# Experts right behind attention: one routing table of 71 tiles with two lists, the last 28 rows routed ahead of them, row buffers that also hold results

## What is computed (the reference, cut)

```
x = x + L0_conv(_ln_c(x))          # gated attention over image rows, 64 channels, 128 x 128, 4 heads of 32
t = _to_tokens(x)                  # 8192 tokens of 128 numbers
t = t + L0_ffn(_ln_t(t))           # 8 experts, 2 for each token

def _L0_ffn_ref(x, Wg, bg, W1, b1, W2, b2):
    gate_logits = xf @ Wg + bg
    top_w, top_i = jax.lax.top_k(gate_logits, 2)
    top_w = jax.nn.softmax(top_w, axis=-1)
    ...
    for e in range(E):
        h = jax.nn.gelu(xf @ W1[e] + b1[e], approximate=False)      # 128 -> 512
        out = out + w_dense[:, e:e + 1] * (h @ W2[e] + b2[e])       # 512 -> 128
```

## Time and profile before

| | |
|---|---|
| runs | 858.76 us median of 3 (855.01 to 860.4) |
| profiled execution | 861.2 us, span 859.0 us, mean granted clock 0.917 |
| busy | PE 670.5 (78%), DVE 632.3 (74%), ACT 614.8 (72%), POOL 418.4 (49%) |
| the chain that ended last | PE 49%, DVE 19%, issue 8%, POOL 8%, ACT 7%, DMA 6% |

### The profile page before, as it was taken

How to read it: one execution, slowest core, us unless ns; L and a number is a source line. 1 busy time by engine, 2 the same in 40 slices (tenths; PEclk the granted TensorE clock), 3 DMA queues, 4 the chain that set the end, 5 groups by cost and what they waited for, 6 DMA issues and landing times.

```text
span 859.0 us, 23093 instructions
## 1 busy us (share of the span) xinstructions
PE 670.5 (78%) x7161; PEld 551.0 (64%) x7162; DVE 632.3 (74%) x2324; ACT 614.8 (72%) x1550; POOL 418.4 (49%) x516
## 2 busy tenths in 40 slices
PE   0098988888999899789885162799888888999980
PEld 0097777776777677677674152587666667888860
DVE  4973688885778987687985557677667767899974
ACT  2673999997998898688897231587767666888860
POOL 7010122235436465445665630177777777566660
PEclk9999999998999998899997555799999999999995
DMA  9968300000000000000011320223223323543557
GB/s 207 266 173 187 56 2 2 2 2 2 2 1 2 2 27 17 12 17 27 27 33 35 94 75 17 44 82 85 84 80 84 89 84 92 159 133 96 159 157 266
DMA packets 65925, 63.97 MB, mean 74 GB/s; under 512 B 21158, under 2 KB 57064, under 8 KB 64298
## 3 DMA queue, kind: packets, MB, share of 16 engines
q1 hardware_dynamic: 54170, 34.90, 16.6%
q0 software_dynamic: 9152, 18.76, 6.5%
q10 hardware_dynamic: 2512, 9.18, 3.9%
HBM read 35.88 MB, written 26.93 MB: 73 GB/s over the span
## 4 chain that ended last, share of the span: by engine, by line
PE 49%; DVE 19%; issue 8%; POOL 8%; ACT 7%; DMA 6%; SPq 1%; ACTq 0%; POOLq 0%; DVEq 0%
PE PT L1552 9%; PE PT L1390 5%; PE S L1378 4%; PE S L1535 3%; POOL expert_out L774 3%; POOL routed L743 3%; PE B L1335 3%; ACT L L850 3%; PE S L1537 3%; PE S L1536 3%; DVE xt L1052 2%; PE B L1420 2%; DVE pl L1017 2%; DMA expert_out<-yo,rows_all 2%; DVE L L1030 2%
## 5 line engine op out<-in xcount | busy, mean ns | idle before, releaser
L774 POOL DMA_INDIRECT expert_out<-yo,rows_all x156 | 156.8, 1005 | 88.5 <-ACT yo L944 51.9
L936 ACT ACTIVATE hf<-S,b_sb,inv_hscale 128x256 f32<-128x256 f32 x312 | 150.5, 562 | 48.7 <-PE S L1537 47.1
L743 POOL DMA_INDIRECT routed<-pay,pos x128 | 125.2, 978 | 83.8 <-issue 32.8
L850 ACT ACTIVATE L<-L,lmin 128x128 f32<-128x128 f32 x512 | 159.5, 392 | 0.4
L1030 DVE CUSTOM_DVE_ANT_0 L<-S,biasN 128x128 f32<-128x128 f32 x512 | 117.2, 284 | 17.2 <-issue 15.8
L1288 DVE SCALAR_TENSOR_TENSOR hl<-hf,hscale,hh 128x512 f16<-128x512 f32 x156 | 117.7, 754 | 5.5
L1286 DVE TENSOR_SCALAR hh<-hf,hscale 128x512 f16<-128x512 f32 x156 | 77.8, 499 | 55.9 <-ACT hf L936 55.7
L705 POOL TENSOR_TENSOR og<-on,rden 128x256 f32<-128x256 f32 x64 | 39.2, 616 | 139.7 <-DVE on L1043 113.5
L845 ACT ACTIVATE ph<-PT 128x512 f16<-128x512 f32 x128 | 75.9, 595 | 29.8 <-PE B L1407 19.5
L1535 PE MATMUL S<-fx_h,w_h 128*128 128x256 f16 x312 | 86.5, 277 | 12.7 <-issue 11.5
L1017 DVE TENSOR_TENSOR pl<-PT,ph 128x512 f16<-128x512 f32 x128 | 84.4, 683 | 9.1 <-ACT ph L845 8.9
(11 more groups left out here) (249 smaller groups left out, 1685.3 us busy)
## 6 DMA issues: line engine op xcount, KB each, us to landing
rows_all<-routed SPq DMA_DIRECT2D x78, 130.0 KB
shared<-expert_out SPq DMA_DIRECT2D x6, 768.0 KB, 5.3
shared<-in_L_ffn_W SPq DMA_DIRECT2D x8, 512.0 KB, 7.3
routed<-blank SPq DMA_DIRECT2D x30, 129.0 KB, 2.3
expert_out<-yo,rows_all POOLq DMA_INDIRECT x156
out<-xt SPq DMA_DIRECT2D x6, 384.0 KB, 5.0
xt<-in_x ACTq DMA_DIRECT2D x4, 512.0 KB, 10.1
xt<-in_x SPq DMA_DIRECT2D x4, 512.0 KB, 15.5
```

Source lines behind the costliest of these rows:

```text
L743: pool.indirect_dma_start(routed[TABLE_OF[b]], bass.IndirectOffsetOnAxis(ap=pos[k][:, row:row + 1], axis=0), source[:, part_row(b, i), :], ...
L774: pool.indirect_dma_start(expert_out, bass.IndirectOffsetOnAxis(ap=row_place[t % IN_BUFS][:, k, W + 1:W + 2], axis=0), yo[t % YO_BUFS][:, ...
L850: last = nc.scalar.activation(L[p][:, h, i, :], L[p][:, h, i, :], ACT.Exp, scale=-1.0, bias=lmin[p][:, h * R + i:h * R + i + 1])
L936: last = nc.scalar.activation(hf[p][:, b, :], S[2 * p + pair][:, k * TILE:(k + 1) * TILE], ACT.Gelu, scale=inv_hscale[:, 0:1], bias=b1_fla ...
```

## The change

- `BATCHES` are 12, 12, 12 and 28 rows. There is one table of 2*64*128/256 + 7 = 71 tiles. Its first 29 tiles are the full tiles of the first 36 rows' lists; their table (`full_table`) is written in attention steps 30 and 31. The other 42 (the rests of these lists, and the tiles with late rows) are written by VectorE behind tile steps 1, 3 and 5.
- POOL's row scales are split over two steps, 8 rows and 4. Scatter quotas change.
- The squares of the weights become eight ACT pieces in attention steps 12 to 19, the scales follow in steps 20 to 25, the high halves are eight pieces in steps 28 to 34, the low halves eight pieces in and behind steps 33 and 34. Scales of rows 36 to 55 and the normalised rows of five late groups move into steps 32 to 34.
- Late rows are turned into six PSUM banks and four buffers; logits are taken at once.
- The experts begin when the last rows have their positions. POOL issues all 56 late scatters ahead of the first send. The second table is waited for at tile 29.
- 23 row buffers (8, and 15 in the memory of `pay0`) hold rows and, after the tile, its results; `yo` is gone. The tile loop is written out; the 12 additions stand behind steps 61 to 72.

```
-    BATCHES = ((0, 16), (16, 12), (28, 12), (40, 24))
-    PART_ROWS = (40, 24)
-    PART_TILES = [2 * n * P // TILE + E - 1 for n in PART_ROWS]
-    TILES = sum(PART_TILES)
+    BATCHES = ((0, 12), (12, 12), (24, 12), (36, 28))
+    ROUTED = sum(n for _, n in BATCHES[:3])
+    LATE = HALF - ROUTED
+    FULL = ROUTED - (E - 1)
+    TILES = 2 * HALF * P // TILE + E - 1
+    REST = TILES - FULL
+    DONE = ROUTED + E - 1
-    IN_BUFS = 8
-    YO_BUFS = 4
+    LOADS = 8
+    IN_BUFS = 23
...
+        rows_in = [rows_all[:, b] for b in range(LOADS)] + [pay[0][:, 2 * b:2 * b + 2, :] for b in range(IN_BUFS - LOADS)]
...
-        BODY = 8
-        LOOPS = (5, 53, 77)
+        ADD_AT = {TILES - 10 + i: divmod(i, 4) for i in range(12)}
...
+        SQUARES_STEP, SCALES_STEP = 12, 21
+        LATE_SCALES = ((ROUTED, 56), (56, HALF))
+        W_HIGH_AT = {28: (0,), 30: (1,), 32: (2,), 33: (3, 4), 34: (5, 6, 7)}
...
-                scale[c] = b
+                scale[c - 1], scale[c] = (b, 0, n - R), (b, n - R, n)
...
-                quota = 2 if s in scale_at else 3 if s in rows_at else 5 if s < UNITS else 8
+                quota = 1 if s in scale_at else 2 if s in pool_rows_at else 5 if s < LAST - 1 else 2 * ROUTED
...
+            load_rows(0, IN_BUFS)
+            sp.wait_ge(counts_ready, 1)
+            for e in range(E):
+                pad_region(e)
+            load_rows(IN_BUFS, FULL)
+            sp.wait_ge(padded, 32 * PADS)
+            sp.wait_ge(table_ready, 2)
+            for k in range(2):
+                sp.wait_ge(scattered[3][k], 16 * BATCHES[3][1])
+            load_rows(FULL, DONE + IN_BUFS)
+            sent_through(sp, DONE - 1)
+            load_first_results(0)
+            load_first_results(1)
+            load_rows(DONE + IN_BUFS, TILES)
...
-                if t + 2 < TILES:
-                    pool.wait_ge(h_full, 2 * (t + 2) + 1)
...
+            pool.wait_ge(copied, 1)
+            for k in range(2):
+                for i in range(BATCHES[3][1]):
+                    scatter_rows(3, k, i)
             for t in range(TILES):
                 send_rows(t)
...
+                if 0 <= s - SQUARES_STEP < 2 * HB:
+                    weight_squares(s - SQUARES_STEP)
+                for j in W_HIGH_AT.get(s, ()):
+                    high_weights(j)
...
+                for part, at in enumerate(((24, "B"), (24, "D"), (25, "B"))):
+                    if (s, place) == at:
+                        weight_scales(part)
+                for part, at in enumerate(((30, "A"), (30, "D"), (31, "D"))):
+                    if (s, place) == at:
+                        full_table(part)
+                for part, at in enumerate(((UNITS, "A"), (UNITS, "B"), (UNITS, "D"))):
+                    if (s, place) == at:
+                        dve.wait_ge(stats_done, LATE_SCALES[0][1] // R)
+                        row_scales(chain, slice(*LATE_SCALES[0]), 1e-5, (part,))
+                for n, at in enumerate(((UNITS + 1, "A"), (UNITS + 1, "B"), (UNITS + 1, "D"), (UNITS + 2, "A"), (UNITS + 2, "A"))):
+                    if (s, place) == at:
+                        normal_rows(FIRST_LATE + n, pay[1])
+                if (s, place) == (UNITS + 1, "D"):
+                    split_weights(0)
+                if (s, place) == (UNITS + 2, "A"):
+                    second_bias()
+                    split_weights(1)
+                    split_weights(2)
...
             statistics(GROUPS - 1)
+            dve.wait_ge(stats_done, GROUPS)
+            row_scales(chain, slice(*LATE_SCALES[1]), 1e-5)
+            normal_rows(GROUPS - 2, pay[1])
+            normal_rows(GROUPS - 1, pay[1])
+            split_weights(3)
+            take_late_logits(A)
             pick(3)
+            split_weights(4)
+            split_weights(5)
+            take_ranks(3, B, 0)
+            positions(3, (0, 1))
+            positions(3, (2,))
+            split_weights(6)
+            split_weights(7)
...
+            after = {1: rest_table_counts, 3: lambda: held.extend(rest_table()), 5: lambda: rest_table_rows(*held)}
+            for s, (g, j) in ADD_AT.items():
+                after[s] = lambda g=g, j=j: add_first(g, j)
+            tile_steps(tile_step, after)
...
-            pe.wait_ge(table_ready, 2)
-            pe.wait_ge(w_split, 2)
-            tile_steps(pe, tile_step)
+            pe.wait_ge(table_ready, 1)
+            tile_steps(tile_step, {})
```

More of the change, by code:

```diff
@@ L55, in wait, with rsqrt @@
     engine.wait_ge(sem, value)
[L58 to L63, removed]
+def rsqrt(nc, chain, y, v, a, b, parts=(1, 2)):
+    if 1 in parts:
+        seed_bits = a.bitcast(I32)
+        chain.link(nc.vector.tensor_scalar(seed_bits, v.bitcast(I32), 1, None, ALU.arith_shift_right))
+        chain.link(nc.vector.tensor_scalar(y.bitcast(I32), seed_bits, -1.0, RSQRT_SEED, ALU.mult, ALU.add))
+    for _ in range((1 in parts) + 2 * (2 in parts)):
         chain.link(nc.vector.tensor_tensor(a, y, y, ALU.mult))
@@ L345, in build @@
         y_ready = sem("y_ready")
-        y_sent = [sem(f"y_sent{b}") for b in range(YO_BUFS)]
+        y_sent = [sem(f"y_sent{b}") for b in range(IN_BUFS)]
         y0_in = [sem(f"y0_in{g}") for g in range(3)]
@@ L392, in rows, with tile_steps @@
             return bass.ds(g0, R)
-        BODY = 8
-        LOOPS = (5, 53, 77)
         BODY_ROWS = 12
-        def tile_steps(engine, step, extra=None):
-            assert LOOPS[2] == TILES - 1 and all((b - a) % BODY == 0 for a, b in zip(LOOPS, LOOPS[1:]))
+        ADD_AT = {TILES - 10 + i: divmod(i, 4) for i in range(12)}
+        def tile_steps(step, after):
             e = None
[L405 to L417, removed]
+            for s in range(-1, TILES + 2):
+                e = step(s, s % 8, e)
+                if s in after:
+                    after[s]()
         def tile_stages(s):
-            if not isinstance(s, int):
-                return True, True, True, True
             return s + 1 < TILES, 0 <= s < TILES, 1 <= s <= TILES, s >= 2
@@ L1169, in positions @@
                         chain.link(nc.vector.tensor_copy(pos[j][:, rows], f))
+                if b == 3 and 2 in pieces:
+                    late_meta(1)
                 if 1 not in pieces:
@@ L1265, in _, with cumulate @@
-            for g in range(10, GROUPS):
-                take_logits(g, B)
-            pick(3)
-            split_weights(0)
-            take_ranks(3, B)
-            positions(3)
-            tile_table(1, carry[4])
-            split_weights(1)
+            def cumulate(a, b, n):
+                at = 0
+                d = 1
+                while d < n:
+                    nc.vector.tensor_copy(b[at % 2][0:1, 0:d], a[0:1, 0:d])
+                    chain.link(nc.vector.tensor_tensor(b[at % 2][0:1, d:n], a[0:1, d:n], a[0:1, 0:n - d], ALU.add))
+                    a, at, d = b[at % 2], at + 1, 2 * d
+                return a
```

501 lines of the change are left out of this document (277 added, 224 removed).

## The result

The changed kernel takes 799.09 us, the median of 4 runs (798.24 to 807.13), against 858.69 us before in the same comparison: 0.9324 of it, 95% interval 0.9287 to 0.9361. The forecast was 782, its range 767 to 804. The profiled execution took 798.93 us, with a span of 797.1 us.

The account below looks back on a forecast made before the run. It took waits on POOL's sends and row loads to bound the first experts, TensorE the second part, with little overlap before them. Terms -3 - 30.2 - 42.1 - 1.8 = -77.1 gave 782 us from a median of 858.76; range 767 to 804.

Parts of the forecast that it names:

- TensorE's line: Experts: 448.0 + 61.8 + 240.3 = 750.1 for the last tile's copy, 760.1 for its result, 762.4 with two sends.
- Rival (a): Experts' end: POOL ends the kernel; at 1.08 us an issue its line ends at 772, the kernel at 792; chance 0.20.
- rival (b): Attention: added pieces are all seen and the clock falls as often as now, +15 us, 797; chance 0.13.
- Part 1: Attention up to step 32: net -3 us, bounds -14 and +12.
- -12 us for what goes: Attention: time saved by splitting POOL's row scales, 5.2 us in two steps shown, as much around the third batch.
- the high pieces: Attention: two high-weights pieces on ACT, 0.9 us each, within 4.5 us added together with first table and weight scales.
- Part 2: Bridge from step 32's copy to the first expert matmul: 61.8 us instead of 92.0, gain 30.2, bounds 24 and 35.
- three covers: Bridge: twelve scatters land before TensorE asks at 503; ACT's high pieces precede VectorE's splits; late payload ready 4.3 us early.
- Part 3: Experts, first matmul to last tile's copy: 240.3 us, gain 42.1, with 3.29 us a tile, table 7.1, additions 4.5.
- POOL's line: POOL from 505.5: 56 scatters and 142 sends at 1.262 us, 249.9, plus 0.35 for each of 12 sends, ending 759.6.
- Part 4: Tail: last result to last issue 2.3 us instead of 4.1, -1.8; then 19.5 us to the end, unchanged.
- Rival (f): POOL's issues: VectorE locks POOL out on most, slower; needs 1.65 us an issue to reach 859; 0.02 with another rival.

Follow-up runs that it names:

- the run with one chain: Changed kernel, but POOL computes the row scales of 12 rows in one chain in one step, not 8 and 4 over two: 794.53 us, ratio 0.9256.
- run with one column: Changed kernel, but each of the 12 additions in the last tiles works on 1 column of a row instead of 128: 795.41 us, ratio 0.9244.

## Why the prediction was right in kind and 17 us short

- **Sum.** Both lines were written down, and the time followed the other one. TensorE's line, forecast to 762.4 with its sends, came to 766.0 + 2.3 = 768.3. POOL's, forecast to 759.6, came to 777.7. The span is 777.7 - 762.4 = 15.3 us longer than forecast; 781.9 became 797.1. The other 2 us are the 2.4 that the forecast took off because the profiled execution before was above its median; after the change it is not (798.93 against 799.09). Rival (a) (POOL ends it, 792, chance 0.20) is what happened, on top of a part of rival (b) (attention grows). The time lies outside the forecast's own 774 to 791, and inside 767 to 804 only because that range took these two rivals in.
- **Part 1 failed.** Forecast -3 up to step 32's copy, measured +6.7 (+7 to +10 counted from step 3's copy, over seven executions' traces). The wrong term is "-12 us for what goes". I read the 15.63 us around the third batch as the scales chain's and took for granted that shorter chains vanish. They do at the first batch: steps 9 to 13 are 3.1 us shorter than before, with the first squares piece among them. Around the third (steps 21 to 25) only 1.3 us went, and steps 14 to 20 became 6.2 and steps 26 to 32 7.3 us longer: 9.1 in sum. Each batch's split adds POOL work (6.0 + 5.3 us for 8 and 4 rows, 6.7 for 12 in the run with one chain), and above all it moves scatters into steps where they wait in front of the gate multiplies. The forecast counted the chains and the quotas' number of scatters, not what each of them waits for. With one chain for the second and third batch, no scatters in steps 22 and 29 and the first high pieces moved, attention lost 9 to 12 us (346.4). Of the added terms the squares were right, 2.4 to 5.1 us (4.5 forecast); the high pieces were 1.3 to 4.0 of the other 4.5, and no run shows the first table and the weight scales apart from them.
- **Part 2 was right.** 59.8 us for 61.8, a gain of 32.2. All three covers held: the twelve scatters ended by 504, the load was there ahead of the tile, the payload was ready 3.5 us ahead of the first matmul (4.3 forecast).
- **Part 3 was right.** 237.5 us for 240.3. The pace was 3.29 us. The table cost 6.8 us (from 525.99 to 555.79, seven tiles; 7.1 forecast), the additions some 1.9 us of TensorE's time (4.5). TensorE waited for no load behind a send.
- **POOL's line: both terms short.** It began 8.6 us later, which is Part 1 again. It was 263.6 us long where 249.9 + 4.2 were forecast. The additions cost it 5.1 us (4.2 forecast, run with one column). The other 8.6 us are tiles' operations: in the changed kernel's trace 39 issues began inside `hh` or `hl` and are 8.7 us longer than 0.96 in sum. The forecast read 0.95 from 728 to 760 as 19.02/20, but the window's edge cuts the last issue; the twenty are 0.99 on average. Most of them are 0.96: POOL waited for results there, and its issues began when no such operation was well under way. In the stretch from 788 to 828 the mean is 1.08, in part from additions (six issues of 1.30), and it stood only in the rival.
- **The rule on shared ports.** The forecast weighed the Trainium skill, SBUF — State Buffer, "SBUF: two separate sides", by which VectorE's two-port mode locks GpSimd out of writing descriptors, and held that the trace agrees for the additions but not for the bulk of VectorE's work. That reading failed. The section calls the pair of ports an exclusive lock: an operation of VectorE in a two-port mode, or with two inputs in SBUF against a GpSimd operation that reads SBUF, or else the GpSimd operation has it for its whole length, whichever starts first. The traces agree: 565 of 565 issues inside `hh`, `hl`, an addition or a piece of low weights waited for its end, 317 of 318 that began less than 0.075 us behind its start did not wait, and 19 issues inside `fx_l`, which reads PSUM, took 0.96. That `hh` as tensor_scalar runs in a two-port mode no row shows. The longest issue of the line is 1.75 us, beside an addition of 1.0; the section's 3100 ns for a DMA overlapped was not approached.
- **Part 4.** 19.4 us from the last issue to the end (19.5 forecast); what stands ahead of it is 11.6 us, not 2.3, because POOL was behind.
- **A sum that doesn't hold.** Rival (f)'s 1.65 us an issue should be 1.55: (839.5 - 576.2)/142 - 0.30. Nothing rests on it.
- **Open.** How much of the lengths of steps 24 and 25 is the first choice's wait, and how much of the gain of one chain is chain and how much is scatters, was not separated: the kernels without these waits differ in the chains too.

## What to carry to other kernels

When two lines arrive together in the sum, the forecast is the later of both with their errors, not the likelier: size the denser one with durations from the densest stretch that the profile has, and ask of each longer one which operation of another engine it began in. A queue in program order has to be read whole for each step: an operation that waits puts its wait on everything behind it, and a change of one quota moves all later work. An experiment that undoes one edit must list what else its plan moves.

## What the runs showed of the hardware

- An indirect DMA on GpSimd takes 0.96 us, with 0.305 to the next, and longer when VectorE is inside certain operations as it begins. Here are the 2574 issues of POOL's line in the thirteen traces of the changed kernel and its variants; "holding" are `hh` in both forms, `hl`, the additions and the pieces of low weights:

```
VectorE at the issue's start                        | what the issue takes (count)
idle                                                | 0.95 to 1.06 (625)
holding, for 0.10 us or more, 0.15 or more left     | until 0.83 to 0.85 behind that operation's end (565)
  of these 0.25 to 0.35 us left                     | 1.08 to 1.18 (113)
           0.35 to 0.45                             | 1.18 to 1.24 (308)
           0.55 to 0.65                             | 1.41 to 1.48 (55)
           0.85 to 1.00                             | 1.68 to 1.75 (11)
holding, for 0.075 to 0.10 us                       | 43 so, 8 of 51 took 0.96
holding, for less than 0.075 us                     | 0.95 to 0.97 (317), one 1.05
inside fx_l (reads PSUM), 0.10 or more, 0.15 left   | 0.95 to 0.96 (19)
```

The form with one input and the two forms with two don't differ in this; what counts is how much of the operation is left. The other issues began near the end of an operation, or beside one of another kind (the table's among them), and were not sorted.

- GpSimd's power costs by the column: 1.04 us for 128x4, 1.67 for 128x8, 2.30 for 128x12 and 2.94 for 128x16, that is 0.41 + 0.16 a column; the other 15 instructions of the chain take 0.29 us each however many rows there are.
